# Softmax sums in one go into the shared ring of banks, a third score bank, and layer 3's weight split off VectorE, in a stack of four attention layers

## The reference

```python
# layer 0: one head, keys of 32 channels
attn = softmax(einsum('bki,bkj->bij', q, k));  x = batchnorm(gamma * einsum('bcj,bij->bci', v, attn) + x)
# layer 1: group norm, one head of 256 channels, output projection, x + out
# layers 2 and 3: group norm, 8 heads of 32 channels
weight = softmax(einsum('bct,bcs->bts', q * scale, k * scale))
a = einsum('bts,bcs->bct', weight, v);  out = einsum('oc,bct->bot', proj_w, a) + proj_b
return xn + out   # layer 2;  layer 3: x + out
```

## Time and profile before

| what | value |
|---|---|
| median of 3 runs | 1860.53 us (1860.29 to 1861.84) |
| profiled execution | 1861.36 us |
| its span | 1859.6 us |
| PE busy | 1673.1 us (90%) |
| DVE busy | 1048.1 us (56%) |
| POOL busy | 1011.9 us (54%) |
| ACT busy | 925.8 us (50%) |

### The profile page before, as it was taken

One profiled execution on the slowest core, in us unless ns is written; L12 is line 12 of the kernel. 1 busy time (PEld: TensorE's weight loads), 2 busy tenths in 40 slices (PEclk: granted clock), 3 DMA queues, 4 the chain that ended last, 5 costly groups with the idle time before them and its releaser, 6 DMA issues.

```text
span 1859.6 us, 25009 instructions
## 1 busy us (share of the span) xinstructions
PE 1673.1 (90%) x8222; PEld 1001.1 (54%) x8222; DVE 1048.1 (56%) x1635; ACT 925.8 (50%) x1487; POOL 1011.9 (54%) x402
## 2 busy tenths in 40 slices
PE   3888869999994789999999997999999999999987
PEld 2666747788883444545545544444454454455522
DVE  2445535454542466667567666675576576656611
ACT  2334414343331246665565564665666566556553
POOL 2323221211213148687677775787688678767764
PEclk7889979999997679999999998999999999999997
DMA  3000000000000330330330320303213123033000
GB/s 140 18 18 1 18 1 1 1 1 1 1 1 23 68 69 1 69 69 1 70 69 1 69 63 24 69 1 74 45 25 69 25 69 69 2 92 70 1 23 23
DMA packets 25000, 67.53 MB, mean 36 GB/s; under 512 B 7200, under 2 KB 8992, under 8 KB 24864
## 3 DMA queue, kind: packets, MB, share of 16 engines
q1 hardware_dynamic: 24864, 65.78, 14.5%
HBM read 7.82 MB, written 4.19 MB: 6 GB/s over the span
## 4 chain that ended last, share of the span: by engine, by line
PE 53%; ACT 4%; SPq 3%; issue 3%; DVE 2%; DMA 1%; POOL 1%; POOLq 0%; ACTq 0%; DVEq 0%
PE psA L952 15%; PE psO L871 12%; PE psD L927 12%; PE psD L79 10%; PE psO L874 4%; ACT PR L1127 3%; SPq L1213 2%; DVE BNS L1004 2%; SPq L1215 2%; DMA QS<-SL 1%; POOL PA L1193 1%; ACT XH L1071 0%; DMA QS<-MROW 0%; PE psD L922 0%; POOL SL L1173 0%
## 5 line engine op out<-in xcount | busy, mean ns | idle before, releaser
L1127 ACT ACTIVATE PR<-psA 128x512 f32<-128x512 f32 x1024 | 582.2, 597 | 480.8 <-PE psA L952 438.1
L1004 DVE TENSOR_REDUCE BNS<-psD 128x1 f32<-128x512 f32 x1024 | 633.5, 683 | 233.8 <-PE psD L927 233.7
L1193 POOL TENSOR_TENSOR PA<-PA,PR 128x2048 f32<-128x2048 f32 x128 | 585.6, 4575 | 16.4 <-ACT PR L1127 4.0
L952 PE MATMUL psA<-QS,KS 97*128 97x512 f32 x1024 | 461.1, 459 | 41.5 <-ACT PR L1127 33.6
L927 PE MATMUL psD<-KS,QS 96*128 96x512 f32 x1024 | 397.8, 429 | 23.4 <-DVE BNS L1004 11.3
L952 PEld LDWEIGHTS psA<-QS,KS 97*128 97x128 f32 x1024 | 191.4, 191 | 351.0 <-ACT PR L1127 199.2
L594 POOL TENSOR_SCALAR P<-P,RS 128x1024 f32<-128x1024 f32 x64 | 72.1, 1126 | 359.3 <-DVE RS L345 359.3
L871 PE MATMUL psO<-PR,V 128*32 128x512 f32 x2048 | 261.4, 618 | 0.7 <-ACT PR L1127 0.7
L927 PEld LDWEIGHTS psD<-KS,QS 96*128 96x128 f32 x1024 | 201.4, 197 | 82.0 <-DVE BNS L1004 37.1
L1193 POOL TENSOR_TENSOR PA<-PR 128x2048 f32<-128x2048 f32 x32 | 146.7, 4585 | 126.0 <-ACT PR L1127 126.0
L1173 POOL TENSOR_TENSOR SL<-SL,SH 128x1024 fp32r<-128x1024 f32 x34 | 80.6, 2373 | 155.2 <-ACT SH L1079 155.2
(11 more groups left out here) (131 smaller groups left out, 1845.7 us busy)
## 6 DMA issues: line engine op xcount, KB each, us to landing
KS<-SH SPq DMA_DIRECT2D x128, 128.0 KB, 2.4
QS<-SH SPq DMA_DIRECT2D x128, 128.0 KB, 2.5
KS<-SL SPq DMA_DIRECT2D x64, 128.0 KB, 2.5
QS<-SL SPq DMA_DIRECT2D x64, 128.0 KB, 2.5
X<-x SPq DMA_DIRECT2D x4, 1024.0 KB, 9.0
out<-X SPq DMA_DIRECT2D x4, 1024.0 KB, 4.3
KH<-KL SPq DMA_DIRECT2D x8, 128.0 KB, 2.4
QH<-KL SPq DMA_DIRECT2D x8, 128.0 KB, 2.4
```

Of the source, the lines that this page charges most:

```text
L952: e.matmul(psA[:, s % 2, :], KS[0:STACK + 1, p, q, j * PART:(j + 1) * PART], QS[0:STACK + 1, p, q, h * HALF:(h + 1) * HALF], start=True, s ...
L1004: top = e.tensor_reduce(MXH[:, h, q, tile:tile + 1], full, AX.X, ALU.max)
L1127: e.activation(PR[:, J % 4, (s % QUADH) * HALF:(s % QUADH + 1) * HALF], psA[:, s % 2, :], ACT.Exp, scale=scale).then_inc(exp_done, 1)
L1193: e.tensor_tensor(PA[:, :], PR[:, (J - 1) % 4, :] if j == 1 else PA[:, :], PR[:, J % 4, :], ALU.add).then_inc(sum_done, 1)
```

## The change

It has four parts.

1. Layer 0's XL, and layer 1's for the first batch, are made by DVE; POOL keeps layer 1's for the other batches. PE asks for XH before a projection and for XL only before its third product, which now comes last over both halves.
2. In layer 1 ACT makes XH from X with scale and bias, once X is batch-normed (`bn_done`), and no longer from XN.
3. The three ones-pieces of a half are one unit z of the ring, at steps 34.9 and 2.9 (of the next phase, for the second half), in the order tile 7, tile 6, PA. The value pieces of tiles 6 and 7 stand together at step 33 (and at step 1 of the next phase). DVE's `take_half` is what takes z. psO's bank 1 is free by that and is a third score bank: a score waits for the exp three steps back (two steps, at the first two steps of an even phase). The maxima run from step 6 to 58 with one hole, 35 to 38.
4. The split of layer 3's weights is done by ACT (WH, after step 12) and by POOL (WL, after its third add).

The diff, cut to its core:

```diff
-                                    e.wait_ge(xl_done, CT * (b + 1))
...
-                                for h in range(2):
-                                    mv = slice(h * HALF, (h + 1) * HALF)
-                                    mm = split_products(e, psD[0:width, slot, mv],
-                                                        [(ww[:, t, cols], xx[:, t, mv])
-                                                         for ww, xx in ((WH, XH), (WL, XH), (WH, XL)) for t in range(CT)])
+                                for k, (ww, xx) in enumerate(((WH, XH), (WL, XH), (WH, XL))):
+                                    if i == 0 and k == 2:
+                                        e.wait_ge(xl_done, CT * (b + 1))
+                                    for h in range(2):
+                                        mv = slice(h * HALF, (h + 1) * HALF)
+                                        for t in range(CT):
+                                            mm = e.matmul(psD[0:width, slot, mv], ww[:, t, cols], xx[:, t, mv],
+                                                          start=(k == t == 0), stop=(k == 2 and t == CT - 1))
                                 mm.then_inc(unit_full, 1)
...
+                            def input_low(b):
+                                for t in range(CT):
+                                    e.wait_ge(xh_done, CT * b + t + 1)
+                                    if L1:
+                                        e.wait_ge(xn_done, CT * b + t + 1)
+                                    src = XN[:, t * N:(t + 1) * N] if L1 else X[:, b, t, :]
+                                    e.tensor_tensor(XL[:, t, :], src, XH[:, t, :].bitcast(F32), ALU.subtract).then_inc(xl_done, 1)
...
                                     e.tensor_scalar(X[:, b, t, :], X[:, b, t, :], BNF[:, t, 0:1], BNF[:, t, 1:2],
-                                                    ALU.mult, ALU.add)
+                                                    ALU.mult, ALU.add).then_inc(bn_done, 1)
...
+                            input_low(0)
...
+                                    if not L1 and i == 4 and more:
+                                        input_low(b + 1)
...
                                     if L1:
-                                        e.wait_ge(xn_done, CT * b + t + 1)
-                                        src = XN[:, t * N:(t + 1) * N]
+                                        e.wait_ge(bn_done, CT * b + t + 1)
+                                        e.activation(XH[:, t, :], X[:, b, t, :], ACT.Identity, scale=SCB[:, t, b, 0:1],
+                                                     bias=SCB[:, t, b, 1:2]).then_inc(xh_done, 1)
...
-                                        src = X[:, b, t, :]
-                                    if b and t == 0:
-                                        e.wait_ge(unit_full, index["v", 1, b - 1] + 1)
-                                    e.activation(XH[:, t, :], src, ACT.Copy).then_inc(xh_done, 1)
+                                        e.activation(XH[:, t, :], X[:, b, t, :], ACT.Copy).then_inc(xh_done, 1)
...
-        M_AT = (5.5, 58)
-        HOLES = [[(35, 39)], [(12, 13.5), (35, 39)]]
+        M_AT = (6, 58)
+        HOLES = [(35, 38)]
         XN_AT = 12
 
-        HALVES_AT = {"v": (0, 1), "w": (3.5, 5), "K": (28, 29.3), "Q": (30.6, 31.9), "p": (14.5, 17.5, 20.5, 23.5)}
+        HALVES_AT = {"v": (0, 1), "w": (3.5, 5), "K": (28, 29.3), "Q": (30.6, 31.9), "p": (14.5, 17.5, 20.5, 23.5),
+                     "z": (34.9, 2.9)}
         BANKS = 4
+        SCORE_BANKS = 3
...
+        def score_bank(s, p):
+
+            i = (s + p) % SCORE_BANKS
+            return psA[:, i, :] if i < 2 else psO[:, 1, :]
...
-        WEIGH = [("av", 0, 13), ("av", 1, 13), ("av", 2, 18), ("av", 3, 18), ("av", 4, 26), ("av", 5, 26),
-                 ("av", 6, 30), ("sum", 6, 30), ("av", 7, 34), ("sum", 7, 34), ("pa", NT, 35)]
...
+        WEIGH = [(0, 13), (1, 13), (2, 18), (3, 18), (4, 26), (5, 26), (6, 33), (7, 33)]
+        PIECES = NT - 1
...
+        def weighed(P, J):
+
+            h, j = J // NT, J % NT
+            return PIECES * 2 * P + PIECES * h + min(j + 1, PIECES)
...
-                    def weigh(P, p, h, kind, j):
...
+                        if j == 0:
+                            wait(e, out_done, 2 * P + h)
+                        wait(e, exp_done, STEPS * P + QUADH * (NT * h + j + 1))
+                        source = PR[:, j % 4, :].rearrange("p (q n) -> p q n", q=QUADH)
                         for q in range(QUADH):
                             cols = slice(CH * q, CH * q + CH)
-                            if kind == "av":
-                                mm = e.matmul(psO[cols, 0, :], V[:, p, j, cols], source[:, q, :],
-                                              start=(j == 0), stop=(j == NT - 1))
-                            else:
-                                mm = e.matmul(psO[cols, 1, :], ones[:, 0:CH], source[:, q, :],
-                                              start=(j == NT - DIRECT), stop=(j == NT))
-                        if (kind, j) in LAST_PIECES:
+                            mm = e.matmul(psO[cols, 0, :], V[:, p, j, cols], source[:, q, :], start=(j == 0), stop=(j == NT - 1))
+                        if j < NT - DIRECT:
                             mm.then_inc(av_done, 1)
...
+                    def sums(full, P, h):
+
+                        for j in (NT - 1, NT - 2, NT):
+                            if j == NT:
+                                wait(e, sum_done, ADDS * (2 * P + h + 1))
+                            source = PA[:, :] if j == NT else PR[:, j % 4, :]
+                            source = source.rearrange("p (q n) -> p q n", q=QUADH)
+                            for q in range(QUADH):
+                                mm = e.matmul(full[CH * q:CH * q + CH, :], ones[:, 0:CH], source[:, q, :],
+                                              start=(j == NT - 1), stop=(j == NT))
+                            if j == NT - 2:
+                                mm.then_inc(av_done, 1)
+                        return mm
...
-                            wait(e, exp_done, STEPS * P + s - 1)
-                            e.matmul(psA[:, s % 2, :], KS[0:STACK + 1, p, q, j * PART:(j + 1) * PART],
+                            wait(e, exp_done, STEPS * P + s - (1 if p == 0 and s < 2 else SCORE_BANKS - 1))
+                            e.matmul(score_bank(s, p), KS[0:STACK + 1, p, q, j * PART:(j + 1) * PART],
                                      QS[0:STACK + 1, p, q, h * HALF:(h + 1) * HALF],
                                      start=True, stop=True).then_inc(st_full, 1)
...
-                    def take_half(P, p, h):
-
-                        wait(e, av_done, (2 * P + h + 1) * NT)
+                    def take_half(full, p, h):
+
                         out_ap = A[:, p, h * HALF:(h + 1) * HALF]
-                        e.transpose(ST[:, :], psO[:, 1, :])
+                        e.transpose(ST[:, :], full).then_inc(vec_free, 1)
...
+                        elif u == "z":
+                            take_half(full, p ^ i, i)
...
+                        if what == "weights":
+                            e.wait_ge(w3_loaded, 16)
+                            e.wait_ge(d_full, units_full(NGRP // 2 - 1, "v"))
+                            e.activation(WH[:, :, :], w3_staged, ACT.Copy).then_inc(w3_high, 1)
...
+                        if layers[0] != layers[1]:
+                            events.append((XN_AT, 0, "weights", 0))
...
+                                wait(e, av_done, weighed(P, J - 4))
                                 if J >= 4:
-                                    wait(e, av_done, 2 * NT * P + J - 3)
                                     h, j = (J - 4) // NT, (J - 4) % NT
                                     wait(e, sum_done, ADDS * (2 * P + h) + min(max(j, 1), ADDS))
                                 else:
-                                    wait(e, av_done, 2 * NT * P + J - 3)
                                     wait(e, sum_done, ADDS * 2 * P)
...
-                            e.activation(PR[:, J % 4, (s % QUADH) * HALF:(s % QUADH + 1) * HALF], psA[:, s % 2, :],
+                            e.activation(PR[:, J % 4, (s % QUADH) * HALF:(s % QUADH + 1) * HALF], score_bank(s, p),
                                          ACT.Exp, scale=scale).then_inc(exp_done, 1)
...
+                                if j > 1:
                                     wait(e, sum_done, ADDS * (2 * P + h) + j - 1)
                                 e.tensor_tensor(PA[:, :], PR[:, (J - 1) % 4, :] if j == 1 else PA[:, :],
                                                 PR[:, J % 4, :], ALU.add).then_inc(sum_done, 1)
                                 if norm is not None and h == 0 and j == 3:
                                     input_low(norm, norm_b, layers[2])
+                                if layers[0] != layers[1] and h == 0 and j == 3:
```

(3 more changed lines are left out.)

107 lines of the change are left out of this document (46 added, 61 removed).

## The result

| | before | changed |
|---|---|---|
| median, same chip | 1860.41 us (1857.44 to 1861.84, 4 runs) | 1807.63 us (1804.76 to 1811.02, 4 runs) |
| profiled execution | 1861.36 us | 1806.44 us |
| its span | 1859.6 us | 1804.6 us |
| granted clock, mean | 0.941 | 0.956 |

The ratio is 0.9719 (95% interval 0.9697 to 0.9741): 2.8% faster, 17.6 us above the forecast and inside its range.

What follows compares the result with a forecast made beforehand. PE and ACT were taken to set each phase's first part, POOL's five adds its second. Terms summed to -70.5 from the profiled 1861.4: 1790.9 profiled, 1790 us in the median, range 1762 to 1832.

Steps and rivals of the forecast that it cites:

- five adds of 4.6 whatever PE does: Second part of each phase, behind the first (exp 0 to exp 39): POOL's adds set its 23.3 us.
- the forecast's own sign of being wrong: Phase borders: the forecast is wrong if something other than POOL's fifth add releases exp 0, such as the row.
- batches of layer 0 (and the clock, -4): Layer 0: projections no longer wait for POOL's XL, three times -3.8, so -11.5; less low clock in those gaps, -4.
- moved pieces and third bank, fifteen phases: Eight-head first parts: pieces moved from step 62 cost +1.7, net -1.8 a phase with the bank; -27 (-52 to +25).
- layer 3's weights: Weights' phase: ACT and POOL replace DVE's split; first part's excess falls from 12.7 to 4 us, -8.5 (-4 to -12).
- last phase and output: Last phase, without maxima: -4 in its first part, -5.9 in its second, taken as -9 together (-2 to -12).
- PE's waits for exps go: First part with the third bank: PE needs 6.2 us, DVE 6.3 over eight steps; no phase gains its whole 11.7 us.
- rival (a): Third bank gives nothing: moved pieces eat PE's lead, DVE sets steady steps, first parts stay; about 1830, chance 0.20.
- DVE's backlog: First part: DVE's delay behind the sums, charged 0.7 us on the way from 41.5 to 43.2.
- the mechanism in layer 0: Gaps between layer 0's batches: granted clock is 0.52 for 7 us where PE stands; closing them may give -4.
- the fear of less clock: Last phase: PE gets less busy and may be granted less clock, so -4 and -5.9 were taken as -9.
- PE's three scores ahead: Weights' phase: with a value block and an output unit they cover 3 of ACT's 7 us of wait and copy.

Runs made afterwards that it cites:

- experiment 9: Two runs: part 4 alone on the kernel before, 1859.33 us (1.0021); the changed kernel with part 4 undone, DVE making the split, 1815.83 us (0.9771).
- parts 1 and 2 alone: The kernel before with only layer 0's and 1's new XL and XH and the third product last, old eight-head part: 1832.28 us (0.9869).
- Experiment 1: The changed kernel with the third score bank taken back, so score s again waits for exp s-2: 1842.93 us (0.9917).
- experiment 3: The changed kernel with five matmuls that nobody reads at the end of each phase, behind step 63: 1814.63 us (0.9759).
- experiment 6: The changed kernel with DVE's maxima taken over 256 of each tile's 512 columns, the matmuls left whole: 1754.87 us (0.9474).

## Why the prediction was right, and where it was not

The second part, "five adds of 4.6 whatever PE does", held in all kernels. That exp 0 stands right behind the fifth add held at twelve of the fifteen borders of the changed kernel, 0.1 us behind it. At the three where a loop jumps back, score 0 was late and released exp 0, 0.6 to 1.1 us behind the add: there the forecast's own sign of being wrong came true. Of the sum's terms:

| term | forecast | measured in the trace |
|---|---|---|
| start | -3.9 | -4.6 |
| batches of layer 0 (and the clock, -4) | -15.5 | -14.5 to the fourth batch's projection, -2.5 behind it |
| layer 1's start; its second batch | -5.0; -1.6 | -5.0; -5.6 |
| moved pieces and third bank, fifteen phases | -27 | -7.3 |
| layer 3's weights | -8.5 | -7.1 (phase 6 in experiment 9) |
| last phase and output | -9 | -8.8 |
| sum | -70.5 | -54.9 |

(The rest of layer 1 and the first group gave 0.4 back. Of the start's 4.6, some 0.7 is no part of the change: x landed sooner, and with parts 1 and 2 alone PE started at 10.76, as forecast. DVE's XL took 1.2 us for each of its two parts, 1.3 forecast. Phase 6 is 8.7 us shorter in all; with DVE's split put back it is still 1.6 shorter, and this 1.6 is counted with the third bank.)

**The step that was mis-sized is the third bank's.** The forecast let "PE's waits for exps go" and came to 43.2 us, with 11.7 us of waits a phase behind it. Those were loads' waits; PE's own were 26.0 us in fifteen phases, 1.7 each. The forecast of -1.8 a phase is 1.7 for the pieces and so -3.5 for the bank. Experiment 1 measured, in the fourteen phases without phase 6, -1.55 for the bank and +1.14 for the rest of part 3. The price of the pieces was no worse than forecast, the lead grew as forecast, and rival (a), "the moved pieces eat PE's lead", is near in its sum, though not in its reason: first parts did not stay as they are. The norm phases gained 1.5 us each, near the 1.8; the phases without a norm lost 1.4.

**DVE was taken at its average.** The forecast set 6.3 us of DVE against 6.2 of PE and charged 0.7 for DVE's backlog. Its first part of 43.2 with the lead of 2.5 makes a way of 45.7 us from score 0 to exp 39. Phases 1 and 5, which have no low clock, took 47.2 and 47.3; with maxima over half of the columns they took 45.8 and 45.9. So some 1.4 us of the way is DVE's maxima, twice what was charged.

**What the forecast did not see is the border.** Taking the pieces from step 62 was priced as work moved into PE's part. That they also kept PE busy while the row is on its way was not. By the profile's waits PE stood 1.1 to 1.4 us ahead of score 0 at every border without a jump, where it had stood not at all at nine of twelve and 0.6 at most, and 3.5 to 3.9 at those with one (1.6 to 1.9 before), and the clock fell at five, 1.6 us each in the two where experiment 3 measured it. With tile 6 back and the loops written out, first parts are 43.8 to 44.2 us without a norm and 50.3 to 51.0 with one, phases 0 and 6 apart (43.2 and 50.5 forecast): much of what was missing lay at the borders. The forecast named the mechanism in layer 0 and did not carry it here. The Trainium skill, TensorE: Matmul & The Clock Gate, Part 1, has the throttled state as the default that activity lifts; experiment 3 agrees (1.00 with the fill, 0.52 without).

**The single heads gave more, by the clock.** After layer 1's first projection the granted clock was 0.61 from 287.2 to 295.0 before, and is 1.00 at the same place now, where 36 matmuls fit into 8.0 us, for 22 into 7.8 (rows of before, then after):

```profile
287.20:295.00 7.80, 7.80 (x22) 6.14 (x23) 1.23 (x1) 1.14 (x2) 0.00 (x0) 0.61 0.00 0
```

```profile
260.00:268.00 8.00, 8.00 (x36) 6.30 (x35) 2.61 (x4) 2.41 (x4) 1.13 (x1) 1.00 0.00 0
```

That is most of the 4 us that the second batch gained beyond its 1.6. What tipped the clock there was not tested.

**The last phase's two terms held, and the fear of less clock did not.** Its first part went from 38.6 to 33.7 us (-4.9, forecast -4; 39.9 with two banks in experiment 1), its second, to the last sum, from 30.5 to 24.9 (24.6 forecast). That is 10.5 us. The forecast took 9 for that fear. It was before that the clock was low in this phase: 0.56 over 14 us, with a value block at 3.64 us; now it is 1.00 and a block is 1.92. How much of the gain is the clock's was not parted. Rows of before, then after:

```profile
1814.00:1828.00 14.00, 13.03 (x43) 3.69 (x42) 0.00 (x0) 6.09 (x12) 13.59 (x3) 0.56 0.00 1
```

```profile
1763.00:1779.40 16.40, 15.73 (x79) 5.28 (x78) 0.17 (x1) 12.18 (x25) 15.80 (x4) 1.00 0.00 1
```

PE now stands 4.35 us for POOL's last add, and behind this stand the output's matmuls take 8.7 us for 7.1, which makes -8.8 in all.

**The weights' term was right only in company**: its "PE's three scores ahead" hold with three banks and not with two (experiment 9). ACT's wait for the copy and its work took 7.1 us, 7 forecast.

## What to carry to other kernels

Don't price a change by the waits of weight loads: they run mostly beside the multiplication ahead of them, here 175 us with 26 in the matmuls' own row, and a third bank took 100 off them for 25 of time. The matmuls' own row is not the whole price either: no matmul waited for DVE by the profile, and shorter maxima took 35 us of PE's busy time. Compare the distance between two fixed points (score 0, exp 39) in a run with the suspect made cheap. Before work is moved out of a place where it seems to cost nothing, ask what the engine does there without it: a stand of 1.1 to 1.2 us for a DMA was followed by TensorE's lower clock in two phases. Where parts of a change share a limit (banks, here), test each in the presence of the others, since a part that gives nothing alone can give 7 to 8 us with them.

## What the hardware showed that I had not expected

- A jump back of PE's loop costs: in the changed kernel score 0 behind it came 4.3 to 4.8 us after the row's DMA was issued, elsewhere 2.1 to 2.3, and 6.7 to 8.1 in five of the six cases in which four or five more matmuls stood ahead of the jump (4.4 in the sixth). Writing the loops out took 12.9 us off the time for three jumps.
- After nearly equal stands (1.14 and 1.22 us by the profile's waits) the clock fell in phases 7 and 9 and not in 1 and 5 (1.21 both), nor in 2, 4, 10, 12 and 14 after 1.3 to 1.4. With the maxima of experiment 6 it did not fall in 7 and 9 either, after 1.14 and 1.23. What decides stays open.
- POOL's subtraction of 1536 columns took 3.48 us and ACT's copy 1.48, where DVE had taken 3.78 and 4.25 beside POOL's work. It was a subtraction of POOL's, not an add, that ran beside DVE's 3.78, and it was slowed too: 3.06 us, 2.36 for the next one of its kind. With DVE's split back in the changed kernel (experiment 9), DVE took 2.42 for the copy and 5.93 for the subtraction, and POOL's add beside the latter 5.02 instead of 4.5.
